# A fused decoder layer with non-local block: on VectorE the lower half of the last key unit ahead of row statistics and of the second row turn

## The chip, the cores and the metric

The kernel runs on one core of a Trainium2 chip. The metric is the device time of one execution in microseconds (us). The kernel before was timed three times: 2006.98, 2008.20 and 2008.48 us, median 2008.2 us.

## The reference

Sixteen sequences of 256 tokens with 512 features go through one decoder layer (masked self-attention, cross-attention over a second input of 256 tokens, a perceptron with 2048 hidden units), 16 heads of 32 each, and then through a non-local block. All arrays are float32.

```python
def layernorm(x, scale, bias):
    m = jnp.mean(x, axis=-1, keepdims=True)
    v = jnp.mean(jnp.square(x - m), axis=-1, keepdims=True)
    return (x - m) * jax.lax.rsqrt(v + EPS) * scale + bias
def attention(q, k, v, mask):
    scores = jnp.einsum('bhqd,bhkd->bhqk', q, k) / jnp.sqrt(jnp.float32(HD))
    scores = scores * mask - 10000.0 * (1.0 - mask)
    probs = jax.nn.softmax(scores, axis=-1)
    return jnp.einsum('bhqk,bhkd->bhqd', probs, v)
ln_out = layernorm(hidden_states, ln1_s, ln1_b)
q, k, v = jnp.split(ln_out @ w_qkv + b_qkv, 3, axis=-1)
ctx = merge_heads(attention(split_heads(q), split_heads(k), split_heads(v), ltor_mask))
x = hidden_states + ctx @ w_ao + b_ao
ln_out = layernorm(x, ln2_s, ln2_b)
q = ln_out @ w_q + b_q
k, v = jnp.split(encoder_states @ w_kv + b_kv, 2, axis=-1)
ctx = merge_heads(attention(split_heads(q), split_heads(k), split_heads(v), cross_mask))
x = x + ctx @ w_co + b_co
ln_out = layernorm(x, ln3_s, ln3_b)
x = x + gelu(ln_out @ w1 + b1) @ w2 + b2
# then, over each of the 16 sequences, a non-local block (1x1 convolutions
# theta, phi, g and w, a batch normalisation and the residual):
W = jnp.einsum('bnc,bcm->bnm', theta_x, phi_x) / phi_x.shape[-1]
y = jnp.einsum('bnm,bmc->bnc', W, g_x).transpose(0, 2, 1)
```

## The kernel before

Every float32 product is made of three: an operand is split into an upper half (names ending in `_h`, rounded by ScalarE) and a lower half (`_l`, what is left, by VectorE or GpSimd), and `product` (L66 to L68) runs high by high, high by low and low by high on TensorE.

**Bodies.** After a first stage (the folded matrices of the non-local block, up to about 80 us) the attention runs in 17 bodies, `body(r, k)` with k = 0 to 16, up to about 1265 us; then comes the perceptron, which the change does not touch. A body works on two sequences (512 tokens): bodies 0 to 7 are the self-attention of the eight pairs, 8 to 15 the cross-attention, and body 16 drains. A body has 8 slots, h = 0 to 7. Each slot carries one group of four heads through each stage of a software pipeline: the scores of one group, masking and maxima of the next older one, exponentials of the one before that, the turn of its probabilities on TensorE, their product with the values, and the division by the row sums.

**Units.** In each slot TensorE also makes two units of projection (`units_at`): in slots 0 to 3 a query unit (`q`, n = h) and a key unit (`k`, n = h), in slots 4 and 6 two value units, in slots 5 and 7 two output units of the body before. Units and weighed values take turns in two PSUM banks (`banks`). The key unit of slot h is the last unit of its slot, and its bank is the one that the first unit of slot h + 1 writes: `occupy` lets TensorE wait for `k_lo`, which VectorE counts up when it has made the lower half `k_l` (L1639), before that first product.

**Order.** Each engine runs its instructions in the order written by its own `slot` function, with semaphores between engines. In one slot (0 to 3):

- TensorE: eight transposes of probabilities (L1071, two heads), three quarters of the query unit, the turn of another head, the rest of the query unit, the key unit, scores (L1055, 24 matmuls), weighed values (L1089).
- VectorE: mask, first half (L1656, waits for the first transposes of the slot); inverse row sums, their turn, division of the weighed values (`scaled`, L1694, which writes `cx` and needs the broadcast inverses `rt` from a DMA); exponentials turned in blocks (L1686); four maxima (L1666, each with its accumulator read); mask, second half; `q_l` (L1639); four more maxima; then the tail of the slot, which the change edits: row statistics, `k_l`, row transposes.
- ScalarE: two exponentials, copies of turned probabilities, then `weighed` (L1375, waits for `scaled`), another exponential, `q_h`, five exponentials, and last `k_h` (L1299), for which `k_l` waits.
- GpSimd waits for the slot's last maximum, then makes the lower half of `cx` and, in some slots, row normalisation (L774), biases and splits.
- SyncE issues most DMAs, among them the way of the inverse row sums to DRAM and back to `rt`; ScalarE's queue carries rows, context and masks.

The row statistics of the next body (`row_statistics`, L1604, two tiles each in slots 0 and 1) are gathered by `aggregate` at the head of slot 2; GpSimd then normalises the rows in slots 2 and 3. The normalised rows of bodies 1 to 14 (`by_blocks`) are transposed in 32 x 32 blocks by VectorE (`dve.transpose` of `x[:, t, :]`, L1814), tiles 0 and 1 in slot 3 and 2 and 3 in slot 4, and written to DRAM from ScalarE's queue in slots 4 and 5 (`write_block`).

```python
    if in_bank[bank] is not None:
        sem_, per_, more_ = in_bank[bank]
        wait(pe, sem_, r * per_ + more_)
```

Of the kernel before, what the change touches and what calls it, by code (L numbers as in the profile page):

```python
# [18 lines left out]
TT = TOK // P  # L19
# [27 lines left out]
def f32(ap):  # L47

    return ap.bitcast(F32)
# [88 lines left out]
def whole_network(nc, ctx, nl, m1t_dram, inv_dram, p_dram, xt_dram, rows, x1, x2, ctx_t, s_mask, x_mask, s_weights, x_weights, fold_wt, columns,  # L138
# [12 lines left out]
    NU = 2 * NB  # L151
# [9 lines left out]
    with ExitStack() as stack:  # L161
# [27 lines left out]
        x = room.sb("x", [P, TT, H])  # L189
# [144 lines left out]
        ln_st, ln_mv, ln_ve, ln_rs, ln_x = (room.sem(n) for n in ("ln_st", "ln_mv", "ln_ve", "ln_rs", "ln_x"))  # L334
# [16 lines left out]
        a_blk, st_a, ld_a = room.sem("a_blk"), room.sems("st_a", 2), room.sems("ld_a", 2)  # L351
# [25 lines left out]
        def exists(k, h, d):  # L377
            return 0 <= NG * k + h - LAG + d < GROUPS
# [27 lines left out]
        def turns_at(k, h):  # L406

            return {6: (0, 1), 7: (2, 3)}.get(h, (None, None)) if k == 0 else (None, None)

        def by_blocks(k):  # L410

            return 0 < k < NU - 1
# [20 lines left out]
        def late(k, h):  # L433

            return (k, h) in ((0, 6), (0, 7))
# [1128 lines left out]
        def _(dve):  # L1564
            def split_raw(c, some):
                part = slice(c * H, (c + 1) * H)
                for t in some:
                    dve.wait_ge(w_hi, c * KT + t + 1)
                    hi, lo = f32(w_h[:, t, part]), w_l[:, t, part]
                    if c < 3:  # L1570
                        factor = lns_q[:, 0, t:t + 1] if c == 0 else vec(0)[:, t:t + 1]
                        dve.scalar_tensor_tensor(lo, raws[c][:, t, :], factor, hi, ALU.mult, ALU.subtract).then_inc(w_lo, 1)
                    else:
                        dve.tensor_tensor(lo, raws[c][:, t, :], hi, ALU.subtract).then_inc(w_lo, 1)
# [17 lines left out]
            def biases_of(c):  # L1592
                dve.wait_ge(folded, (c + 1) * KT)
                second, part = (1, 0) if c == 3 else (0, c)
                dve.tensor_tensor(bias_sum[:, second, part, :], shifted[:, c, :], vec(4 + c), ALU.add)\
                    .then_inc(bias_ok, 1)
                if part == 0:
                    dve.wait_ge(bias_ok, c + 1)
                    dve.tensor_scalar(bias_q[:, second, :], bias_sum[:, second, 0, :], scale, None, ALU.mult)\
                        .then_inc(bias_q_ok, 1)  # L1600

            def row_statistics(r, t):
                dve.wait_ge(ld_x[t], (r + 1) * DMA)
                last = dve.bn_stats(stats[:, t, :], x[:, t, :])  # L1604
                if t == TT - 1:
                    last.then_inc(ln_st, 1)
# [134 lines left out]
            def step(n):  # L1741
# [29 lines left out]
                if n in (7, 11, 15):  # L1771
                    biases_of((n - 7) // 4)

            def slot(r, k, h, a_, b_, own, pv):
                even, odd = turns_at(k, h)
                coming, leaves = exists(k, h, 1), exists(k, h, -2)
                if k == 0 and h == 0:
                    split_raw(2, range(KT))
                if coming:
                    mask_scores(r, k, h, 0)  # L1780
                if own:
                    inverses(r, h)
                if 0 < k < NU and h == 2:
                    aggregate(r + 1)
                bare = k == NU and h < 2
                if bare:
                    mask_scores(r, k, h, 1)
                if leaves and not late(k, h):
                    scaled(r, h, pv)
                if exists(k, h, 0) and moved(group(r, h, 0)[0]):  # L1790
                    exponentials_in_blocks(r, h)
                if coming:
                    maxima(r, k, h, 0)
                if leaves and k == NU:
                    weighed(r, k, h)
                if coming and not bare:
                    mask_scores(r, k, h, 1)
                if leaves and late(k, h):
                    scaled(r, h, pv)
                if not (k == NU and h == EARLY - 1):  # L1800
                    unit_out(a_, r, k)
                if coming:
                    maxima(r, k, h, 1)
                if even is not None:
                    rows_turned(r + (k < NU), even, tp[:, 0, :])
                    rows_turned(r + (k < NU), odd, tp[:, 1, :])
                if halves_at(k, h) is not None:
                    lower_pair(k, r, halves_at(k, h))
                if k == NU and h in (0, 2):
                    lower_pair(k - 1, r - 1, h // 2)  # L1810
                if by_blocks(k) and h in (3, 4) or k == NU - 1 and 3 <= h < 3 + TT:
                    for t in (2 * h - 6, 2 * h - 5) if by_blocks(k) else (h - 3,):
                        dve.wait_ge(ln_x, (r + 1) * TT + (t + 1))
                        dve.transpose(x[:, t, :], x[:, t, :]).then_inc(a_blk, 1)  # L1814
                if k < NU and h in ((0, 1) if k else (1, 2)):
                    row_statistics(r + 1, 0 if h == (0 if k else 1) else 2)
                    row_statistics(r + 1, 1 if h == (0 if k else 1) else 3)
                if k == 0 and h == 2:
                    aggregate(r + 1)
                if k in (2, 3) and h in (2, 4):  # L1820
                    shift_through(3 * KT + 2 * k - 4 + h // 4)
                if k == 3 and h == 5:
                    biases_of(3)
                if not (k == NU and h == EARLY):
                    for n in m_chunk_at.get((k, h), ()):
                        split_m_chunk(n)
                if k == NU and h == EARLY - 1:
                    activated(0, 0, True)
                    activated(0, 1, True)
                    unit_out(a_, r, k)  # L1830
                unit_out(b_, r, k)
                if k == 1 and h in O_SPLITS:
                    split_raw(3, O_SPLITS[h])
                for n in chunk_at.get((k, h), ()):
                    split_chunk(n)
                if k == NU and h == EARLY:
                    early_chunks = m_chunk_at[(k, h)]
                    for f in range(2, EARLY):
                        if f >= 4:
                            split_m_chunk(early_chunks[f - 4])  # L1840
                        activated(0, f, True)
                    for n in early_chunks[2:]:
                        split_m_chunk(n)
                    dve.wait_ge(m1_hi, 1)
                    dve.tensor_tensor(thw_l[:, :], m1[:, :], f32(thw_h[:, :]), ALU.subtract).then_inc(m1_lo, 1)
# [160 lines left out]
```

## Time and profile before

| | |
|---|---|
| median of three runs | 2008.2 us |
| profiled execution | 2011.13 us, of which the span 2009.3 us |
| TensorE busy | 1976.2 us (98% of the span) |
| VectorE busy | 1470.8 us (73%) |
| ScalarE busy | 1162.6 us (58%) |
| GpSimd busy | 550.2 us (27%) |
| granted TensorE clock | 0.999 over the span |

The profiled execution stands 2.9 us over the median of the runs, 1.8 us of it outside the span. The busy shares of VectorE and ScalarE are averages over two stages: in the page's 40 slices VectorE stands at 9 tenths or 8 from the third to the twenty-fifth slice (the attention) and at 3 to 6 tenths behind them. An operation's "took" overlaps the next one's start by some tens of ns, so distances are read from start to start.

### The profile page before, as it was taken

What the parts mean: (1) busy time and instruction counts of PE and PEld (TensorE: products, weight loads), DVE (VectorE), ACT (ScalarE), POOL (GpSimd) and SP (SyncE); (2) the same over time, 40 slices, a digit from 0 to 9 for tenths busy, and PEclk for the clock granted to TensorE, in tenths of its full rate; (3) what the DMA queues carried; (4) which work ended last, traced back from release to release, by engine and by line L of the source; (5) the groups of instructions that cost most, each with busy time, mean ns of one, the idle gap of its engine ahead of it and who ended that gap; (6) DMA issues with size and microseconds to landing.
All of it is one profiled execution on the core that took longest, in us unless ns stands there. A gap on an engine that the chain in (4) does not pass through costs nothing. (4 is left out here: it accounts for less than half of the span.)

```text
span 2009.3 us, 41550 instructions
## 1 busy us (share of the span) xinstructions
PE 1976.2 (98%) x13632; PEld 1570.0 (78%) x13632; DVE 1470.8 (73%) x3868; ACT 1162.6 (58%) x3251; POOL 550.2 (27%) x556
## 2 busy tenths in 40 slices
PE   9999999999999999999999998999999999999998
PEld 8877777777776777777777776888888888888887
DVE  7799999999999999899899888564444343435333
ACT  4388878888888888888888788421111121212111
POOL 1012222222224344323423432053132131313000
PEclk9999999999999999999999999999999999999999
DMA  8546667567668867767767734531212212121201
GB/s 279 168 94 139 146 165 155 128 168 161 135 173 193 195 172 173 168 162 180 176 152 183 170 90 116 171 107 35 79 42 68 68 47 78 47 63 52 61 24 48
DMA packets 681720, 252.67 MB, mean 126 GB/s; under 512 B 533312, under 2 KB 626112, under 8 KB 681536
## 3 DMA queue, kind: packets, MB, share of 16 engines
q1 hardware_dynamic: 535616, 195.84, 38.5%
q10 hardware_dynamic: 145920, 54.55, 11.2%
q8 instruction: 95, 1.56, 0.3%
q14 instruction: 89, 0.73, 0.1%
HBM read 167.41 MB, written 82.84 MB: 125 GB/s over the span
## 5 line engine op out<-in xcount | busy, mean ns | idle before, releaser
L1309 ACT ACTIVATE A_p<-A_p,A_nmax 128x256 f32<-128x256 f32 x1024 | 507.1, 500 | 5.4 <-DVE A_res L1634 1.7
L1666 DVE CUSTOM_DVE_ANT_0 A_p<-A_p,A_ma 128x256 f32<-128x256 f32 x1024 | 376.6, 423 | 4.6
L1656 DVE TENSOR_TENSOR A_p<-A_sc,A_mk 128x1024 f32<-128x1024 f32 x256 | 312.3, 1220 | 48.0 <-PE A_tp L1071 47.4
L820 POOL TENSOR_TENSOR A_ct_l<-A_cx,A_ct_h 128x256 fp32r<-128x256 f32 x122 | 114.3, 937 | 652.3 <-DVE A_nmax L1666 639.1
L1368 ACT ACTIVATE A_pt<-A_tp 128x512 f32<-128x512 f32 x396 | 218.5, 588 | 47.2 <-PE A_tp L1071 45.9
L1071 PEld LDWEIGHTS A_tp<-A_ident,A_p 128*128 128x128 f32 x1584 | 178.8, 141 | 71.2 <-ACT A_p L1309 33.0
L1071 PE MATMUL A_tp<-A_ident,A_p 128*128 128x128 f32 x1584 | 222.5, 277 | 1.5 <-DVE A_xt_l L1617 0.7
L1505 ACT ACTIVATE A_mk<-A_tp,A_cols 128x512 f32<-128x512 f32 x62 | 42.8, 690 | 269.1 <-PE A_tp L68 269.0
L1309 ACT ACTIVATION_READ_ACCUMULATOR A_p<-A_p,A_nmax 128x1 f32 x1024 | 197.2, 193 | 0.0
L1505 ACT ACTIVATE A_ma<-A_tp,A_cols 128x512 f32<-128x512 f32 x62 | 42.8, 690 | 242.5 <-PE A_tp L68 242.5
L66 PE MATMUL A_banks<-A_xt_h,A_w_h 128*128 128x512 f32 x384 | 162.2, 422 | 3.4 <-DVE A_res L1634 2.1
L929 POOL TENSOR_TENSOR A_v<-A_v,A_b_row 128x512 f32<-128x512 f32 x32 | 52.7, 1664 | 362.3 <-DMA A_v<-x 362.3
L68 PE MATMUL A_banks<-A_xt_h,A_w_l 128*128 128x512 f32 x384 | 151.1, 394 | 0.0
L67 PE MATMUL A_banks<-A_xt_l,A_w_h 128*128 128x512 f32 x384 | 150.1, 391 | 0.0
L1857 DVE CAST A_h_h<-A_ma 128x512 fp32r<-128x512 f32 x64 | 30.5, 476 | 160.4 <-ACT A_ma L1505 156.7
L1375 ACT ACTIVATE A_cx<-A_cx,A_bias_sum 128x256 f32<-128x256 f32 x128 | 65.2, 510 | 139.8 <-DVE A_cx L1694 139.7
L66 PE MATMUL A_tp<-A_xt_h,A_w_h 128*128 128x512 f32 x368 | 143.4, 390 | 0.2 <-DVE A_xt_l L1871 0.2
L67 PE MATMUL A_tp<-A_xt_l,A_w_h 128*128 128x512 f32 x368 | 143.2, 389 | 0.0
L68 PE MATMUL A_tp<-A_xt_h,A_w_l 128*128 128x512 f32 x368 | 143.2, 389 | 0.0
L1089 PE MATMUL A_banks<-A_pt,A_v 128*32 128x256 f32 x2048 | 137.9, 387 | 4.8 <-DMA A_pt<-exponentials 2.1
L1857 DVE CAST A_h_h<-A_mk 128x512 fp32r<-128x512 f32 x64 | 29.1, 454 | 143.6 <-ACT A_mk L1505 141.5
L66 PE MATMUL A_banks<-A_w_h,A_ct_h 128*128 128x512 f32 x256 | 105.7, 413 | 1.6 <-issue 1.1
(248 smaller groups left out, 5001.7 us busy)
## 6 DMA issues: line engine op xcount, KB each, us to landing
exponentials<-A_ln_shift SPq DMA_DIRECT2D x464, 64.0 KB, 2.7
A_pt<-exponentials SPq DMA_DIRECT2D x116, 256.0 KB, 3.1
A_rt<-inverses SPq DMA_DIRECT2D x512, 32.0 KB, 2.4
x<-A_res SPq DMA_DIRECT2D x64, 256.0 KB, 3.6
A_res<-x ACTq DMA_DIRECT2D x58, 256.0 KB, 4.1
turned<-A_x ACTq DMA_DIRECT2D x224, 64.0 KB, 2.8
A_x<-x SPq DMA_DIRECT2D x54, 256.0 KB, 3.7
A_x<-x ACTq DMA_DIRECT2D x42, 256.0 KB, 3.1
```

What stands on the lines that cost most here:

```text
L66: pe.matmul(out, sh, mh, start=first, stop=False)
L67: pe.matmul(out, sh, ml, start=False, stop=False)
L68: return pe.matmul(out, sl, mh, start=False, stop=last)
L820: pool.tensor_tensor(ct_l[:, f, part], cx[:, :], f32(ct_h[:, f, part]), ALU.subtract).then_inc(c_lo, 1)
L1071: last = pe.transpose(tp[:, n % 2, c * S + t * P:c * S + (t + 1) * P], p[:, g % 2, j, t, c * P:(c + 1) * P], ident[:, :])
L1089: last = pe.matmul(banks[rr, bank, 0:S], v[:, b * TPB + c, f * P + j * HD:f * P + (j + 1) * HD], turned_keys(grp, j, c), start=(c == 0), s ...
L1309: act.activation(p[:, g % 2, j, t, :], p[:, g % 2, j, t, :], ACT.Exp, scale=-1.0, bias=nmax[:, g % 2, j, t:t + 1], accum_out=rsum[:, g % 2 ...
L1368: act.activation(pt[:, moved(grp) + i, :, :], tp[:, n % 2, :].rearrange("p (c s) -> p c s", c=TPB), ACT.Copy)\
L1375: act.activation(cx[:, :], cx[:, :], ACT.Identity, bias=bias_sum[:, layer(k, h, -2), 2, f:f + 1]).then_inc(c_sum, 1)
L1505: act.activation(hf[f % 4], hidden_bank(blk, f), ACT.Gelu_apprx_tanh, bias=b1_col[:, f:f + 1])\
L1656: dve.tensor_tensor(p[:, g % 2, heads, :, :].rearrange("p j t s -> p j (t s)"), sc[:, heads, :], m, ALU.mult)\
L1666: dve.tensor_tensor_reduce(out=a_, in0=a_, in1=ma[:, b, t, :], scale=-1.0, scalar=BIG, op0=ALU.add, op1=ALU.min, accum_out=nmax[:, g % 2, ...
```

## The change

Only VectorE's order changes. In bodies 1 to 15 the two row statistics of slots 0 and 1 stand behind `k_l` instead of ahead of it. In slot 3 of bodies 1 to 14 the transpose of row tile 0 stays ahead of `k_l`, that of tile 1 goes behind it. In slot 4 the transposes of tiles 2 and 3 go behind the slot's second unit, which is a value unit and has no work on VectorE; only in body 1 do they pass something, the splits of the output weights (`split_raw`, L1574). Body 0 and body 15's row transposes are as before. No instruction is added or removed, and the four other engines keep their order.

```diff
--- before.py
+++ after.py
@@ -1771,6 +1771,11 @@
                 if n in (7, 11, 15):
                     biases_of((n - 7) // 4)
 
+            def row_blocks(r, t):
+
+                dve.wait_ge(ln_x, (r + 1) * TT + (t + 1))
+                dve.transpose(x[:, t, :], x[:, t, :]).then_inc(a_blk, 1)
+
             def slot(r, k, h, a_, b_, own, pv):
                 even, odd = turns_at(k, h)
                 coming, leaves = exists(k, h, 1), exists(k, h, -2)
@@ -1808,13 +1813,11 @@
                     lower_pair(k, r, halves_at(k, h))
                 if k == NU and h in (0, 2):
                     lower_pair(k - 1, r - 1, h // 2)
-                if by_blocks(k) and h in (3, 4) or k == NU - 1 and 3 <= h < 3 + TT:
-                    for t in (2 * h - 6, 2 * h - 5) if by_blocks(k) else (h - 3,):
-                        dve.wait_ge(ln_x, (r + 1) * TT + (t + 1))
-                        dve.transpose(x[:, t, :], x[:, t, :]).then_inc(a_blk, 1)
-                if k < NU and h in ((0, 1) if k else (1, 2)):
-                    row_statistics(r + 1, 0 if h == (0 if k else 1) else 2)
-                    row_statistics(r + 1, 1 if h == (0 if k else 1) else 3)
+                if by_blocks(k) and h == 3 or k == NU - 1 and 3 <= h < 3 + TT:
+                    row_blocks(r, h - 3)
+                if k == 0 and h in (1, 2):
+                    row_statistics(r + 1, 2 * h - 2)
+                    row_statistics(r + 1, 2 * h - 1)
                 if k == 0 and h == 2:
                     aggregate(r + 1)
                 if k in (2, 3) and h in (2, 4):
@@ -1831,6 +1834,12 @@
                 unit_out(b_, r, k)
                 if k == 1 and h in O_SPLITS:
                     split_raw(3, O_SPLITS[h])
+                if 0 < k < NU and h in (0, 1):
+                    row_statistics(r + 1, 2 * h)
+                    row_statistics(r + 1, 2 * h + 1)
+                if by_blocks(k) and h in (3, 4):
+                    for t in (1,) if h == 3 else (2, 3):
+                        row_blocks(r, t)
                 for n in chunk_at.get((k, h), ()):
                     split_chunk(n)
                 if k == NU and h == EARLY:
```

VectorE in slot 0 of body 7, from the last maxima to the next slot's `scaled`, before (`A_stats` row statistics, `A_k_l` the key unit's lower half, `A_p<-A_sc,A_mk` the next slot's mask):

```order
L1666 ISA A_p,A_nmax<-A_p,A_ma 128x256
L1666 ISA A_nmax 128x1
L1604 BN_STATS A_stats<-A_x 128x6 x2
L1639 SCALAR_TENSOR_TENSOR A_k_l<-A_banks,A_bias_sum,A_k_h 128x512
L1656 TENSOR_TENSOR A_p<-A_sc,A_mk 128x1024
L1673 RECIPROCAL A_rinv<-A_rsum 128x8
L1676 STREAM_TRANSPOSE A_turned_inv<-A_rinv 128x32
L1694 TENSOR_TENSOR A_cx<-A_banks,A_rt 128x256
```

The same place of the changed kernel:

```order
L1666 ISA A_p,A_nmax<-A_p,A_ma 128x256
L1666 ISA A_nmax 128x1
L1639 SCALAR_TENSOR_TENSOR A_k_l<-A_banks,A_bias_sum,A_k_h 128x512
L1604 BN_STATS A_stats<-A_x 128x6 x2
L1656 TENSOR_TENSOR A_p<-A_sc,A_mk 128x1024
L1673 RECIPROCAL A_rinv<-A_rsum 128x8
L1676 STREAM_TRANSPOSE A_turned_inv<-A_rinv 128x32
L1694 TENSOR_TENSOR A_cx<-A_banks,A_rt 128x256
```

The two statistics have changed places with `k_l`; the mask of the next slot still follows both.

VectorE in slot 3 of body 7, before (`A_x<-A_x` the row transposes):

```order
L1666 ISA A_p,A_nmax<-A_p,A_ma 128x256
L1666 ISA A_nmax 128x1
L1814 STREAM_TRANSPOSE A_x<-A_x 128x512 x2
L1639 SCALAR_TENSOR_TENSOR A_k_l<-A_banks,A_bias_sum,A_k_h 128x512
L1656 TENSOR_TENSOR A_p<-A_sc,A_mk 128x1024
L1673 RECIPROCAL A_rinv<-A_rsum 128x8
```

and after the change:

```order
L1666 ISA A_p,A_nmax<-A_p,A_ma 128x256
L1666 ISA A_nmax 128x1
L1777 STREAM_TRANSPOSE A_x<-A_x 128x512
L1639 SCALAR_TENSOR_TENSOR A_k_l<-A_banks,A_bias_sum,A_k_h 128x512
L1777 STREAM_TRANSPOSE A_x<-A_x 128x512
L1656 TENSOR_TENSOR A_p<-A_sc,A_mk 128x1024
L1673 RECIPROCAL A_rinv<-A_rsum 128x8
```

One transpose has gone behind `k_l`, one stays ahead of it.

## Rows read from the trace of the kernel before

**Rows 1.** Waits of the whole program: engine, line <- releaser: us, times, longest.

```profile
PEld A_banks L66 <- DVE A_k_l L1639: 10.1, 16, 1.0
...
DVE A_k_l L1639 <- ACT A_k_h L1299: 8.9, 16, 1.8
```

**Rows 2.** Timeline of VectorE, body 7, slots 0 to 3: start, took, operation, [idle].

```profile
574.18 1.28 DVE L1604 BATCH_NORM_STATS2 A_stats<-A_x 128x6 f32<-128x512 f32 x2
575.38 0.74 DVE L1639 SCALAR_TENSOR_TENSOR A_k_l<-A_banks,A_bias_sum,A_k_h 128x512 fp32r<-128x512 f32 x1
576.03 1.23 DVE L1656 TENSOR_TENSOR A_p<-A_sc,A_mk 128x1024 f32<-128x1024 f32 x1
...
585.02 1.23 DVE L1656 TENSOR_TENSOR A_p<-A_sc,A_mk 128x1024 f32<-128x1024 f32 x1
...
592.89 0.75 DVE L1639 SCALAR_TENSOR_TENSOR A_k_l<-A_banks,A_bias_sum,A_k_h 128x512 fp32r<-128x512 f32 x1 [0.47 <-ACT A_k_h L1299]
593.92 1.23 DVE L1656 TENSOR_TENSOR A_p<-A_sc,A_mk 128x1024 f32<-128x1024 f32 x1 [0.29 <-PE A_tp L1071]
...
601.44 1.30 DVE L1814 STREAM_TRANSPOSE A_x<-A_x 128x512 f32<-128x512 f32 x2
602.66 0.70 DVE L1639 SCALAR_TENSOR_TENSOR A_k_l<-A_banks,A_bias_sum,A_k_h 128x512 fp32r<-128x512 f32 x1
603.29 1.21 DVE L1656 TENSOR_TENSOR A_p<-A_sc,A_mk 128x1024 f32<-128x1024 f32 x1
```

**Rows 3.** Timeline of ScalarE, body 7, slots 0 to 2.

```profile
574.02 0.68 ACT L1299 ACTIVATE A_k_h<-A_banks,A_bias_sum 128x512 fp32r<-128x512 f32 x1
...
578.05 0.51 ACT L1375 ACTIVATE A_cx<-A_cx,A_bias_sum 128x256 f32<-128x256 f32 x1 [1.03 <-DVE A_cx L1694]
...
587.31 0.51 ACT L1375 ACTIVATE A_cx<-A_cx,A_bias_sum 128x256 f32<-128x256 f32 x1 [1.30 <-DVE A_cx L1694]
```

**Rows 4.** Timeline of TensorE, body 7: turns, and the first product after them.

```profile
575.24 1.09 PE L1071 MATMUL A_tp<-A_ident,A_p 128*128 128x128 f32 x8
576.17 0.50 PE L66 MATMUL A_banks<-A_xt_h,A_w_h 128*128 128x512 f32 x1
...
593.13 1.09 PE L1071 MATMUL A_tp<-A_ident,A_p 128*128 128x128 f32 x8
593.98 0.48 PE L66 MATMUL A_banks<-A_xt_h,A_w_h 128*128 128x512 f32 x1
...
602.03 1.09 PE L1071 MATMUL A_tp<-A_ident,A_p 128*128 128x128 f32 x8
603.42 0.50 PE L66 MATMUL A_banks<-A_w_h,A_xt_h 128*128 128x512 f32 x1 [0.30 <-DVE A_k_l L1639]
```

**Rows 5.** Timeline of TensorE, body 14, start of slot 4.

```profile
1114.46 1.09 PE L1071 MATMUL A_tp<-A_ident,A_p 128*128 128x128 f32 x8
1116.35 0.50 PE L66 MATMUL A_banks<-A_w_h,A_et_h 128*128 128x512 f32 x1 [0.79 <-DVE A_k_l L1639]
```

**Rows 6.** Timeline of VectorE, body 14, slot 3.

```profile
1108.87 0.42 DVE L1694 TENSOR_TENSOR A_cx<-A_banks,A_rt 128x256 f32<-128x256 f32 x1 [0.91 <-DMA A_rt<-inverses]
```

**Rows 7.** Timeline of TensorE: body 1, slot 5, then body 7, slot 5.

```profile
179.16 0.47 PE L66 MATMUL A_banks<-A_w_h,A_ct_h 128*128 128x512 f32 x1 [1.08 <-issue]
...
620.07 0.39 PE L1055 MATMUL A_sc<-A_k_h,A_q_h 32*128 32x256 f32 x4 [0.73 <-DVE A_p L1656]
```

**Rows 8.** Timeline of VectorE, body 15, slot 2.

```profile
1180.04 0.75 DVE L1639 SCALAR_TENSOR_TENSOR A_k_l<-A_banks,A_bias_sum,A_k_h 128x512 fp32r<-128x512 f32 x1 [0.90 <-ACT A_k_h L1299]
```

**Rows 9.** Timeline of GpSimd, body 7, slots 3 and 5.

```profile
595.22 1.53 POOL L774 TENSOR_SCALAR A_x<-A_x,A_nmean,A_rstd 128x512 f32<-128x512 f32 x2
...
616.16 1.30 POOL L831 TENSOR_TENSOR A_w_l<-A_wst,A_w_h 128x512 fp32r<-128x512 f32 x1
```

**Rows 10.** Timeline of VectorE, body 7, slot 5.

```profile
616.80 0.94 DVE L1666 CUSTOM_DVE_ANT_0 A_p<-A_p,A_ma 128x256 f32<-128x256 f32 x1
```

## The prediction

> **What bounds the kernel now.** I read the page first: TensorE is busy 98% of the span, so a change on VectorE can only act through the few us in which TensorE waits, or by making more of them. The second view is the list of waits: the weight loads of the first product of a slot waited 10.1 us in 16 places for `k_l`, the longest 1.0 us [rows 1]. That is what the moved order could win. The same list says that `k_l` itself already waits for ScalarE's `k_h` in 16 places, 8.9 us [rows 1], which is what moving it forward runs into. So the third view is the timelines of three engines side by side in one regular body (7), to see who paces whom.
>
> TensorE's first product of a slot starts 0.85 us after the slot's first turns where nothing holds it (593.13 to 593.98). By that measure it is late by 0.08 us at the start of slot 1 (575.24 to 576.17) and by 0.54 us at the start of slot 4 (602.03 to 603.42) [rows 4]. So the place where statistics are moved costs TensorE almost nothing now, and the place where a transpose is moved costs half a us.
>
> ScalarE waits 1.03 us and 1.30 us for VectorE's `scaled` in slots 1 and 2 [rows 3], and from there runs without a gap to `k_h`: from 587.31 on ScalarE to 592.89, where `k_l` starts after 0.47 us of idle time put down to `k_h`, is 5.58 us [rows 2, 3]. In slot 0 `k_h` runs from 574.02 for 0.68 us, to 574.70 [rows 3]; the maxima are over when the statistics start, at 574.18 [rows 2]. The statistics thus fill a hole of some 0.5 us that `k_l` would have to wait through anyway.
>
> **Statistics behind `k_l`, slots 0 to 2.** The pair of statistics costs 1.20 us (574.18 to 575.38), `k_l` to the next mask 0.65 us (575.38 to 576.03) [rows 2], and the mask to ScalarE's wait for `scaled` 2.02 us in slot 1 (576.03 to 578.05) and 2.29 us in slot 2 with the aggregation (585.02 to 587.31) [rows 2, 3].
> - Before, statistics and the wait for `k_h` lay beside each other. After, they stand in one line, and a loop closes between the two engines: `scaled`, 5.58 us of ScalarE, `k_l` 0.65, statistics 1.20, mask to `scaled` 2.02, in sum 9.45 us, against a slot of TensorE of 8.90 to 9.00 us (from 576.03 to 585.02 the masks are 8.99 apart [rows 2]).
> - Slot 0: `k_l` starts at 574.73 instead of 575.38, the next mask at 576.58 instead of 576.03 (+0.55).
> - Slot 1: the loop adds as much again. ScalarE gets `scaled` at 578.60, `k_l` starts at 584.18, the mask of slot 2 at 586.03 instead of 585.02 (+1.01). TensorE wins its 0.08 us at each of two slots and is otherwise untouched, since `k_l` still ends before it is asked for.
> - Slot 2 has no statistics, but everything in it is late by 1.01: `k_l` starts at 593.90 instead of 592.89 and ends at 594.65. TensorE, ready at 593.90, starts its first product of slot 3 at 594.70 instead of 593.98. **TensorE loses 0.72 us here, once per body**, where it lost nothing.
>
> **One transpose behind `k_l`, slot 3.** The two transposes cost 1.22 us (601.44 to 602.66) [rows 2], so 0.61 us goes from ahead of `k_l` to behind it. VectorE starts slot 3 at 594.55 instead of 593.92 (+0.63); `k_l` therefore starts at 602.68 against 602.66: nothing won. If slot 3's `scaled` waits for the broadcast inverses, whose DMAs are triggered in slot 2 and so come a full 1.01 late, `k_l` is late by 1.01 - 0.61 = 0.40. That wait exists: 0.91 us in body 14 [rows 6]. TensorE's own time is +0.72 less what it waits now: in body 7 0.72 - 0.54 = +0.18 us; the later of the two decides. The wait that it has now at the start of slot 4, read as in body 7, is 0.67, 0.64, 0.08, 0.21, 0.45, 0.44, 0.54, 0.83, 0.38, 1.03, 1.04, 0.56, 0.71 and 1.04 us in bodies 1 to 14 (body 14 is 1114.46 to 1116.35 less 0.85 [rows 5]); their sum of 8.6 us is most of the 10.1 of the list [rows 1].
> - Bodies 3 to 14, no late inverses: 0.72 less that wait, never under 0: 0.64 + 0.51 + 0.27 + 0.28 + 0.18 + 0.34 + 0.16 + 0.01 = +2.4 us.
> - With late inverses, never under 0.40: 0.64 + 0.51 + ten times 0.40 = +5.2 us. I take 4.7, nearer to this end, because the wait of [rows 6] is the nearest row and it grows with its trigger.
> - Body 2 I count as 0: its slot 2 carries other work of VectorE ahead of `k_l`.
>
> **What is queued behind.** VectorE starts slot 4 late by 0.65 to 1.0 (the second transpose now comes between `k_l` and the mask). ScalarE, the inverses' DMAs and GpSimd follow it. In most bodies slots 4 to 6 hide that: scores and the first product there wait for VectorE with some spare time, and I cost it at nothing; without the cover it would be up to 0.65 a body. Two bodies have no cover:
> - Body 7, slot 5: the scores already wait 0.73 us for the mask [rows 7], so VectorE's whole lateness of 0.64 to 1.04 arrives, +0.5 to +0.65 over the share counted above; I take 0.5.
> - Body 1: the first product of slot 5 already waits for the split output weights (1.08 us idle [rows 7]), made by ScalarE and then VectorE. The split now stands ahead of two transposes, which would free it 1.2 us earlier, but its upper half comes from ScalarE, which is itself 1.0 late. 0 to +1.1; I take 0.8.
>
> Body 15 keeps its transposes and gets the statistics move: in slot 2 its `k_l` already waits 0.90 us for ScalarE [rows 8], so lateness goes through. +0.7, with 0 as the other end.
>
> GpSimd's normalisation in slot 3 of body 7 ends at 596.75 [rows 9], just ahead of VectorE's maxima. Where the two meet a maximum stretches: 0.94 us at 616.80 beside a GpSimd operation that runs from 616.16 to 617.46, instead of some 0.4 [rows 9, 10]. GpSimd is late by 1.01, VectorE by 0.63 to 1.0, so at most 0.3 us of meeting, which the 0.40 above covers. The Trainium skill, "SBUF — State Buffer", in its section "SBUF: two separate sides", has an exclusive lock for this: a VectorE operation with two SBUF inputs and a GpSimd operation that reads SBUF exclude each other for the whole instruction. By that rule bodies without late inverses would lose up to 0.3 instead of 0; by a mere shared bandwidth nothing to speak of. The stretched maximum agrees with the lock.
>
> **The sum.** 4.7 + 0 + 0.5 + 0.8 + 0.7 = +6.7 us; I take +6.5. Lower bound 2.4 + 0 + 0.5 + 0 + 0 = 2.9, upper 5.2 + 0.65 + 1.1 + 0.7 = 7.7. The profiled execution would go from 2011.1 to 2017.6; it stands 2.9 us over the median of the runs, so the forecast for the median is 2008.2 + 6.5 = **2014.7 us**.
>
> **Rivals.**
> - *The wait for `k_l` simply shrinks (faster).* Were `k_h` ready when the maxima end, the wait at slot 4 would lose up to 0.61 in each of 14 bodies: with the waits above 6.9 us, plus about 0.1 a body at slots 1 and 2 and 1.0 once, 9 us in all: 1999 us. It decides as soon as ScalarE's `k_h` ends before VectorE's last maximum. For it: the list of waits names `k_l` as TensorE's largest. Against it: the 574.70 against 574.18 above, the same in slots 0 and 1 of the bodies I looked at. The Trainium skill, "Perfetto Trace Analysis", section on optimization strategy, would have one find what the gaps of the limiting engine wait for and make it start sooner. By that rule the change is right; the trace says that the thing to start sooner is `k_h`.
> - *It is hidden (no change).* The loop of 9.45 us runs for only two slots; if slot 2 had 1 us to give, TensorE would lose nothing there and slot 4's wait would shrink a little: between 2005 and 2011, say 2008. Slot 2 has 0.34 us only (592.89 + 0.75 against 593.98 [rows 2, 4]), so it needs ScalarE to catch up, which its gapless 5.58 us speak against.
> - *The lateness runs on through slots 4 to 7 (much slower).* With late masks there each body loses up to another 0.65: +10 on top, 2024 us. Against it are the waits that VectorE has there.
>
> **Chances.** Forecast 0.68, faster rival 0.08, hidden 0.17, running on 0.07. Range 2009 to 2019: the bounds 2.9 and 7.7 put the forecast's own at 2011.1 to 2015.9, and I widen it towards the hidden and the running-on case. A measurement of this kernel tells about 0.2% (4 us) from no change. Slower by more: most of the forecast's mass and the running-on case, 0.71; within it 0.21, faster 0.08.
>
> **What the changed profile would show.** Right: `k_l` in slots 0 and 1 waits about 0.5 us for `k_h`, in some 45 places instead of 16; masks of slots 1 and 2 late by 0.55 and 1.0 against TensorE's turns; a new wait of TensorE of about 0.8 us at the start of slot 3; the wait at the start of slot 4 about as late as before. Wrong: no idle time ahead of `k_l` in slot 0 (the hole was not there), or TensorE starting slot 3 0.85 us after its turns (the loop did not add up), or the wait at slot 4 gone without one at slot 3.

## The result and the profile after

The changed kernel takes 2017.4 us (median of six runs, 2015.8 to 2018.4) against 2008.1 us for the kernel before (six runs, 2007.0 to 2011.5). The ratio is 1.0038, with a 95% interval of 1.0028 to 1.0048: slower by about 7.6 us (5.6 to 9.6). The profiled execution took 2018.4 us, of which the span is 2016.6 us. TensorE's busy time went from 1976.2 to 1978.8 us, so of the 7.3 us by which the span grew 4.7 are waiting. One execution of the changed kernel with the earlier `k_h` (4534 us) and one of the kernel before beside it (2438 us) were far longer than their neighbours; they stand in no ratio below.

The list of waits of the changed kernel (engine, line <- releaser: us, times, longest):

```profile
ACT A_cx L1375 <- DVE A_cx L1694: 153.8, 123, 3.9
...
DVE A_k_l L1639 <- ACT A_k_h L1299: 23.7, 46, 1.8
...
DVE A_cx L1694 <- DMA A_rt<-inverses: 15.4, 25, 1.9
...
PEld A_banks L66 <- DVE A_k_l L1639: 10.0, 26, 0.9
...
PE A_sc L1055 <- DVE A_p L1656: 8.3, 20, 1.6
```

`k_l` waits for ScalarE's `k_h` in 46 places instead of 16 [rows 1]. TensorE's weight loads wait for `k_l` just as long in sum as before (10.0 against 10.1 us), but in 26 places instead of 16: the sum of the row did not move, its places did. Only the timelines show that. VectorE in body 7, slots 0 to 3 and the start of slot 4 (start, took, operation, [idle]); it answers to [rows 2]:

```profile
579.77 0.75 DVE L1639 SCALAR_TENSOR_TENSOR A_k_l<-A_banks,A_bias_sum,A_k_h 128x512 fp32r<-128x512 f32 x1 [0.46 <-ACT A_k_h L1299]
580.43 1.28 DVE L1604 BATCH_NORM_STATS2 A_stats<-A_x 128x6 f32<-128x512 f32 x2
581.63 1.21 DVE L1656 TENSOR_TENSOR A_p<-A_sc,A_mk 128x1024 f32<-128x1024 f32 x1
...
589.21 0.75 DVE L1639 SCALAR_TENSOR_TENSOR A_k_l<-A_banks,A_bias_sum,A_k_h 128x512 fp32r<-128x512 f32 x1 [0.47 <-ACT A_k_h L1299]
...
591.07 1.21 DVE L1656 TENSOR_TENSOR A_p<-A_sc,A_mk 128x1024 f32<-128x1024 f32 x1
...
598.90 0.75 DVE L1639 SCALAR_TENSOR_TENSOR A_k_l<-A_banks,A_bias_sum,A_k_h 128x512 fp32r<-128x512 f32 x1 [0.47 <-ACT A_k_h L1299]
...
608.13 0.71 DVE L1639 SCALAR_TENSOR_TENSOR A_k_l<-A_banks,A_bias_sum,A_k_h 128x512 fp32r<-128x512 f32 x1
608.76 0.70 DVE L1777 STREAM_TRANSPOSE A_x<-A_x 128x512 f32<-128x512 f32 x1
609.38 1.18 DVE L1656 TENSOR_TENSOR A_p<-A_sc,A_mk 128x1024 f32<-128x1024 f32 x1
```

ScalarE in the same stretch, which answers to [rows 3]:

```profile
583.63 0.51 ACT L1375 ACTIVATE A_cx<-A_cx,A_bias_sum 128x256 f32<-128x256 f32 x1 [1.45 <-DVE A_cx L1694]
...
588.50 0.67 ACT L1299 ACTIVATE A_k_h<-A_banks,A_bias_sum 128x512 fp32r<-128x512 f32 x1
...
593.33 0.51 ACT L1375 ACTIVATE A_cx<-A_cx,A_bias_sum 128x256 f32<-128x256 f32 x1 [2.21 <-DVE A_cx L1694]
```

Read together they give the loop. From the mask of slot 1 (581.63) to ScalarE's `weighed` (583.63) is 2.00 us, from there to `k_l` (589.21) 5.58, and from `k_l` to the next mask (591.07) 1.86: 9.44 us, and the mask of slot 1 to that of slot 2 is 9.44 us as well. Before it was 8.99 [rows 2]. ScalarE now waits 1.45 and 2.21 us for `scaled` instead of 1.03 and 1.30 [rows 3].

TensorE in body 7, from the turns of slot 2 to the first product of slot 4; it answers to [rows 4]:

```profile
589.29 1.09 PE L1071 MATMUL A_tp<-A_ident,A_p 128*128 128x128 f32 x8
590.14 0.48 PE L66 MATMUL A_banks<-A_xt_h,A_w_h 128*128 128x512 f32 x1
...
596.55 0.39 PE L1055 MATMUL A_sc<-A_k_h,A_q_h 32*128 32x256 f32 x4 [0.19 <-DVE A_p L1656]
...
598.46 1.09 PE L1071 MATMUL A_tp<-A_ident,A_p 128*128 128x128 f32 x8
599.71 0.50 PE L66 MATMUL A_banks<-A_xt_h,A_w_h 128*128 128x512 f32 x1 [0.15 <-DVE A_k_l L1639]
...
607.78 1.09 PE L1071 MATMUL A_tp<-A_ident,A_p 128*128 128x128 f32 x8
608.89 0.50 PE L66 MATMUL A_banks<-A_w_h,A_xt_h 128*128 128x512 f32 x1
```

Slot 2 is now 9.17 us long (589.29 to 598.46) instead of 8.90, because its scores wait for the late second mask, and the first product of slot 3 comes 1.25 us after the turns instead of 0.85. That is 0.27 + 0.40 = 0.67 us at the start of slot 3. At the start of slot 4 the distance is 1.11 us instead of 1.39 [rows 4]: 0.28 us came back. This repeats: in bodies 3 to 14 the distance at slot 3 is 1.24 to 1.30 us everywhere (0.85 before), and the excess over 0.85 at slot 4 sums to 2.7 us against 7.3 before.

From TensorE's turns, body by body, this is how much later the changed kernel is at the start of a body, in the one profiled execution of each: body 1 set to 0, body 2 +2.3, body 3 +0.9, body 7 +2.3, body 11 +4.8, body 15 +5.2, body 16 +5.4. Another 2.5 us lie ahead of body 1, where the two kernels have the same instructions, and behind the start of body 16 the changed kernel is 0.6 us shorter: 7.3 us of span in all. At the start of body 1 the ten further profiled executions stand from 0.2 us earlier to 2.9 us later than the first one of the kernel before, the unchanged kernel at +0.05, so I take the 2.5 us for chance of the execution. The unchanged kernel profiled again also had bodies 1 to 15 in 1092.7 us instead of 1095.1: against that trace the changed kernel's 1100.5 us are 7.7 us more, not 5.4. A body's term under some 0.5 us is not settled by one pair of traces unless it comes back in other bodies or kernels.

### The profile page after: what moved, and what is told of

It is laid out like the page before. It is cut to its first block and busy times, and to the rows that moved or that the text cites. A ratio compares the mean times of both kernels' runs of the same rounds, so it can differ in the third digit from the quotient of the medians.

```text
span 2016.6 us, 41550 instructions
## 1 busy us (share of the span) xinstructions
PE 1978.8 (98%) x13632; PEld 1568.8 (78%) x13632; DVE 1467.4 (73%) x3868; ACT 1160.3 (58%) x3251; POOL 549.9 (27%) x556
```

## The experiments

Ten kernels ran. The kernel before was timed beside them: median 2009.9, 2009.7 and 2009.1 us, which is what the ratios stand on; differences in us are these ratios times the 2008 us of before. The unchanged kernel run as an experiment of its own is the measure of the noise.

> The kernel before, unchanged, for the spread of its stages. In the two traces at hand the stage ahead of body 1, which has the same instructions in the same order in both, is 2.5 us longer in the changed kernel. If that is chance of an execution, it will differ by 1 to 3 us here too while the time is that of before; if it belongs to the changed kernel, this trace's body 1 starts at 131.7 us within 0.3.

Measured: 2010.0 us, ratio 0.9998 [0.9988, 1.0007]. Its body 1 starts at 131.79 us, within the 0.3 us of 131.7 that I had named as the sign against chance. By my own test the 2.5 us would belong to the changed kernel. One more execution was too small a test: over all twelve profiled executions body 1 starts between 131.5 and 134.7 us, and one of the later kernels (134.67) starts it later than the changed kernel (134.27).

### The statistics alone

```diff
-                if k < NU and h in ((0, 1) if k else (1, 2)):
-                    row_statistics(r + 1, 0 if h == (0 if k else 1) else 2)
-                    row_statistics(r + 1, 1 if h == (0 if k else 1) else 3)
+                if k == 0 and h in (1, 2):
+                    row_statistics(r + 1, 2 * h - 2)
+                    row_statistics(r + 1, 2 * h - 1)
...
+                if 0 < k < NU and h in (0, 1):
+                    row_statistics(r + 1, 2 * h)
+                    row_statistics(r + 1, 2 * h + 1)
```

> The kernel before with only the statistics of slots 0 and 1 moved behind k_l; all row transposes stay as before. My theory (a loop of 9.45 us: scaled, ScalarE to k_h, k_l, statistics, mask; VectorE late by 1.0 us in slot 2): TensorE waits about 0.8 us more for slot 3's first product, and since both transposes still stand ahead of k_l in slot 3, slot 4's first product is late by the whole lateness, 0.6 to 1.0 us in each of 14 bodies: 2008 + 9 to 14 us, about 2019 us, slower than the full change. The rival that statistics behind k_l cost nothing and the loss lies in the transposes: 2006 to 2009 us. k_l waits for k_h about 0.47 us in slots 0, 1 and 2 of nearly every body.

Measured: 2021.9 us, ratio 1.0059 [1.0046, 1.0072], +11.9 us. The waits of this kernel, and TensorE at the start of slot 4 in body 7:

```profile
DVE A_k_l L1639 <- ACT A_k_h L1299: 23.9, 46, 2.1
...
PEld A_banks L66 <- DVE A_k_l L1639: 18.5, 31, 1.0
```

```profile
609.23 1.09 PE L1071 MATMUL A_tp<-A_ident,A_p 128*128 128x128 f32 x8
611.12 0.50 PE L66 MATMUL A_banks<-A_w_h,A_xt_h 128*128 128x512 f32 x1 [0.79 <-DVE A_k_l L1639]
```

The same 46 waits for `k_h` as in the changed kernel, and the new wait at slot 3 (0.39 to 0.46 us at the first product in each of bodies 1 to 14), but nothing comes back at slot 4: here 1.89 us from the turns, and over bodies 1 to 14 the excess over 0.85 there sums to 11.5 us against 8.6 in the kernel before. The statistics are the loss.

### The transposes alone

The changed kernel with the statistics of bodies 1 to 15 back ahead of `k_l`; the transposes stay where the change put them.

```diff
-                if 0 < k < NU and h in (0, 1):
-                    row_statistics(r + 1, 2 * h)
-                    row_statistics(r + 1, 2 * h + 1)
```

> The changed kernel with the statistics put back ahead of k_l: only the second row transpose of slot 3 (and those of slot 4) is moved. My theory: k_l starts 0.5 to 0.6 us earlier in slot 3, where k_h is ready (slot 3's two transposes outlast it); TensorE's wait at the start of slot 4 shrinks by up to 0.61 us in 14 bodies, 6.9 us in all, some of it given back by the later splits: about 2002 us. The rival that the transpose behind k_l only moves the lateness into the next slot: 2006 to 2009 us.

Measured: 2003.9 us, ratio 0.9967 [0.9954, 0.9980], -6.6 us. Its list of waits has

```profile
DVE A_k_l L1639 <- ACT A_k_h L1299: 8.6, 16, 1.6
...
PEld A_banks L66 <- DVE A_k_l L1639: 2.0, 5, 1.0
```

So with the statistics in place one transpose behind `k_l` removes nearly the whole wait of slot 4: 2.0 us in 5 places instead of 10.1 in 16 [rows 1]. The two halves add to +5.3 us, against +7.6 (5.6 to 9.6) for both together, so within the noise nothing is left over.

### Is it the wait for `k_h`?

If the hole ahead of `k_l` is the cause, an earlier `k_h` must cure the changed kernel without touching VectorE. ScalarE's `k_h` goes ahead of the slot's last exponential in bodies 1 to 15:

```diff
+                ahead = b_ is not None and b_[0][0] == "k" and 0 < k < NU
                 if now:
-                    for n in (5, 6, 7):
+                    for n in (5, 6):
                         exponential(r, k, h, n)
+                    if ahead:
+                        unit_out(b_, k)
+                    exponential(r, k, h, 7)
...
-                unit_out(b_, k)
+                if not ahead:
+                    unit_out(b_, k)
```

> The changed kernel, with ScalarE making k_h ahead of its last exponential of the slot instead of behind it (bodies 1 to 15, slots 0 to 3). My theory: k_h is ready 0.49 us sooner, the loop takes 8.96 us instead of 9.45 and fits TensorE's slot; k_l's waits in slots 0 and 1 fall to about 0, TensorE's new wait at slot 3 goes, and the transposes' gain stays: 2001 to 2004 us. If the loss had another cause than the wait for k_h (statistics in the way of the next mask as such), the time stays near 2016.

Measured: 2004.9 us, ratio 0.9973 [0.9964, 0.9982], -5.4 us against before where the changed kernel has +7.6. VectorE of this kernel in body 7 (`k_l` is L1644 here, the mask L1661), behind the waits:

```profile
DVE A_k_l L1644 <- ACT A_k_h L1299: 3.5, 5, 2.0
```

```profile
571.63 0.75 DVE L1644 SCALAR_TENSOR_TENSOR A_k_l<-A_banks,A_bias_sum,A_k_h 128x512 fp32r<-128x512 f32 x1
...
573.49 1.21 DVE L1661 TENSOR_TENSOR A_p<-A_sc,A_mk 128x1024 f32<-128x1024 f32 x1
...
582.43 1.21 DVE L1661 TENSOR_TENSOR A_p<-A_sc,A_mk 128x1024 f32<-128x1024 f32 x1
```

No idle time ahead of `k_l`, and the masks are 8.94 us apart instead of 9.44: the loop is open, with the statistics still behind `k_l`. The median is 0.9 us over the 2001 to 2004 expected; the kernel before beside it was itself at 2009.9, and the ratio puts it at 2002.8 on the 2008.2 us of before. The same edit on the kernel before is the control:

> The kernel before with ScalarE's k_h ahead of its last exponential, and nothing else. My theory: in slots 0, 1 and 3 k_l stands behind statistics or transposes that outlast k_h, so nothing moves there; slot 2's wait of 0.47 us goes, where TensorE was not waiting: 2007 to 2010 us, no change against before. The rival that k_h is late everywhere and its earlier copy is a gain by itself: 2002 to 2004 us, as in the changed kernel with it.

Measured: 2008.6 us, ratio 0.9998 [0.9989, 1.0006]. There the statistics filled the hole already, so the earlier `k_h` is worth nothing; its place is worth 13.0 us in one order of VectorE and 0.4, which is nothing that can be told, in the other.

### How much filler is enough

The changed kernel with one statistic ahead of `k_l` and one behind it in slots 0 and 1:

```diff
+                if 0 < k < NU and h in (0, 1):
+                    row_statistics(r + 1, 2 * h)
...
                 if 0 < k < NU and h in (0, 1):
-                    row_statistics(r + 1, 2 * h)
                     row_statistics(r + 1, 2 * h + 1)
```

> The changed kernel with one statistic of slots 0 and 1 put back ahead of k_l and the other left behind it. My theory: the one ahead (0.6 us) fills the wait for k_h (0.47 us), the loop takes 9.45 - 0.60 = 8.85 us and fits TensorE's slot of 8.90; k_l waits for k_h hardly at all in slots 0 and 1, masks are not late, and TensorE also wins the 0.08 us at slots 1 and 2: like the turn-only kernel or 1 to 2 us less, 2001 to 2004 us. If each statistic behind k_l cost in proportion (half of the 12 us of the statistics-only kernel): about 2008 to 2010 us.

Measured: 2003.5 us, ratio 0.9970 [0.9958, 0.9982]. VectorE in body 7:

```profile
572.92 0.69 DVE L1604 BATCH_NORM_STATS2 A_stats<-A_x 128x6 f32<-128x512 f32 x1
573.53 0.73 DVE L1639 SCALAR_TENSOR_TENSOR A_k_l<-A_banks,A_bias_sum,A_k_h 128x512 fp32r<-128x512 f32 x1
574.18 0.68 DVE L1604 BATCH_NORM_STATS2 A_stats<-A_x 128x6 f32<-128x512 f32 x1
574.78 1.22 DVE L1656 TENSOR_TENSOR A_p<-A_sc,A_mk 128x1024 f32<-128x1024 f32 x1
```

One statistic (0.61 us from start to start) covers the hole of 0.47 us, and the rest of the slot is on time. Together with the earlier `k_h` nothing more is won:

> The kernel of one statistic on each side, with ScalarE's k_h ahead of its last exponential as well. My theory: the loop is already short enough, so the earlier k_h buys nothing more: within 1.5 us of that kernel, 2000 to 2004 us. If k_h still set the pace anywhere, 2 to 4 us less.

Measured: 2003.3 us, ratio 0.9969 [0.9957, 0.9981].

### One slot instead of two: a miss

The changed kernel with slot 1's statistics back ahead of `k_l`, slot 0's behind it.

```diff
+                if 0 < k < NU and h == 1:
+                    row_statistics(r + 1, 2)
+                    row_statistics(r + 1, 3)
...
-                if 0 < k < NU and h in (0, 1):
+                if 0 < k < NU and h == 0:
```

> The changed kernel with slot 1's two statistics put back ahead of k_l; slot 0's stay behind. My theory (lateness adds up once per slot with statistics behind k_l): VectorE is late by 0.55 instead of 1.01 us in slot 2, TensorE's wait at slot 3 is about 0.3 instead of 0.8 us, and the transpose moved in slot 3 outweighs it in most bodies: 2004 to 2008 us, far below the middle between the changed kernel (2017) and the turn-only kernel (2004). If the cost were simply per moved statistic, that middle: 2010 to 2011 us.

Measured: 2010.6 us, ratio 1.0003 [0.9994, 1.0012]. I expected 2004 to 2008 (the ratio makes it 2008.8 on the 2008.2 us of before); the number of the rival, 2010 to 2011, came out. VectorE was late by 0.42 us in slot 2 of body 7 where I expected 0.55, and slot 3's wait of about 0.3 us did not come: the first product there stands 0.85 us behind the turns in 13 of 14 bodies. The loss is in slot 2, where I had not looked. VectorE and then TensorE of this kernel in body 7, slots 1 and 2:

```profile
578.83 1.21 DVE L1656 TENSOR_TENSOR A_p<-A_sc,A_mk 128x1024 f32<-128x1024 f32 x1
...
587.06 0.73 DVE L1639 SCALAR_TENSOR_TENSOR A_k_l<-A_banks,A_bias_sum,A_k_h 128x512 fp32r<-128x512 f32 x1
```

```profile
586.50 1.09 PE L1071 MATMUL A_tp<-A_ident,A_p 128*128 128x128 f32 x8
587.85 0.49 PE L66 MATMUL A_banks<-A_xt_h,A_w_h 128*128 128x512 f32 x1 [0.26 <-DVE A_k_l L1639]
```

Slot 0 makes VectorE late by 0.45 us. In slot 1 `k_l` stands behind its statistics again and has no spare time (it held TensorE up by 0.08 us already in the kernel before, [rows 4]), so the first product of slot 2 comes 1.35 us after the turns: 0.5 us. It is 0.49 to 0.62 us in bodies 1 to 14 (1.03 in body 8), 7.9 us in all, and that is about the whole distance in the traces to the kernel with the transposes alone (bodies 1 to 15 in 1094.9 against 1087.0 us). A cost per moved statistic does not explain it: the kernel with one statistic on each side has two of the four behind `k_l` as well and loses nothing. In these kernels lateness costs at once where the next `k_l` has filler ahead of it (0.5 us), and a slot later where it has none, as in the changed kernel (0.67 us).

### Slot 4's transposes, and the best version

In body 1 the change also puts a split of the output weights ahead of two transposes. Both kernels here put slot 4's transposes back; the first is otherwise the one with a statistic on each side, the second the changed kernel with the earlier `k_h`.

```diff
+                if by_blocks(k) and h == 4:
+                    row_blocks(r, 2)
+                    row_blocks(r, 3)
...
-                if by_blocks(k) and h in (3, 4):
-                    for t in (1,) if h == 3 else (2, 3):
-                        row_blocks(r, t)
+                if by_blocks(k) and h == 3:
+                    row_blocks(r, 1)
```

> The kernel with one statistic on each side of k_l, and slot 4's two transposes back in their old place, ahead of the second unit and of body 1's splits; slot 3's transpose stays moved. My theory of body 1: with the transposes behind the splits VectorE stands 1.2 us waiting for ScalarE's upper half and ScalarE then 1.3 us for the transposes; put back, body 1 ends 1.1 to 1.4 us sooner than in the kernel it is made from, and no other body changes: 2001.5 to 2003 us. If body 1's loss came from the statistics, nothing changes: 2003.5 us.

> The changed kernel with ScalarE's k_h ahead of its last exponential and slot 4's transposes back in their old place. The same theory: body 1 about 1.2 us shorter than in the kernel with the earlier k_h alone, 2002 to 2004 us; the two statistics behind k_l cost nothing once k_h comes earlier, so it stands within 1.5 us of the kernel with one statistic on each side.

Measured: 2003.7 us, ratio 0.9970 [0.9957, 0.9983], and 2001.8 us, ratio 0.9966 [0.9954, 0.9978]. I expected 2001.5 to 2003 and 2002 to 2004, and neither median tells slot 4's order apart from its pair (2003.5 and 2004.9 us). The traces do: body 1 takes 73.0 us instead of 74.6, and 72.6 instead of 74.2, 1.6 us less in both pairs where I expected 1.1 to 1.4. Over all twelve kernels body 1 lasts 74.0 to 75.6 us in the six kernels with the transposes behind the split, and 72.6 to 73.3 us in five of the six that have them ahead (the sixth, with the statistics alone moved, has 74.2). Body 1, slot 4 of the changed kernel, VectorE, then ScalarE:

```profile
181.10 1.29 DVE L1574 TENSOR_TENSOR A_w_l<-A_wst,A_w_h 128x512 fp32r<-128x512 f32 x2 [1.23 <-ACT A_w_h L1268]
182.31 1.30 DVE L1777 STREAM_TRANSPOSE A_x<-A_x 128x512 f32<-128x512 f32 x2
```

```profile
183.41 0.51 ACT L1309 ACTIVATE A_p<-A_p,A_nmax 128x256 f32<-128x256 f32 x1 [1.32 <-DVE A_x L1777]
```

and the kernel with one statistic on each side and slot 4 as before:

```profile
179.12 1.30 DVE L1777 STREAM_TRANSPOSE A_x<-A_x 128x512 f32<-128x512 f32 x2
180.41 1.29 DVE L1574 TENSOR_TENSOR A_w_l<-A_wst,A_w_h 128x512 fp32r<-128x512 f32 x2
```

It is the pattern of slots 0 and 1 again: the transposes filled a wait of 1.2 us for ScalarE, and moved behind it they make the writes of ScalarE's queue and its next exponential wait 1.3 us. TensorE pays in slot 6 of body 1, at the product of weighed values. In the changed kernel, and then in the one with a statistic on each side and slot 4 moved:

```profile
199.95 1.07 PE L1089 MATMUL A_banks<-A_pt,A_v 128*32 128x256 f32 x16 [1.33 <-ACT A_v L1301]
```

```profile
197.86 1.07 PE L1089 MATMUL A_banks<-A_pt,A_v 128*32 128x256 f32 x16 [1.47 <-DMA A_pt<-exponentials]
```

A wait of 0.85 to 1.47 us stands at this product in all six kernels with slot 4's transposes moved, and in none of the six with them in their old place. In four of the six its releaser is named as the DMA that brings turned exponentials back, in the other two as ScalarE's `v`. The landing of that DMA decides it: the product starts 0.24 or 0.25 us after it in all six, while in the six kernels without the wait the product starts 1.2 us before the same `v` is done, so it does not need it. The path there can be followed in the traces. VectorE, late behind the split, turns the next exponentials 5.1 us after the start of slot 5 instead of 3.9 to 4.1, and SyncE issues their stores from 5.8 us on instead of 4.6 to 4.8. It issues the load at 11.9 to 12.2 us instead of 10.7 to 11.1, and the load takes 7.0 to 7.5 us instead of 5.4 to 6.9. Why it takes longer is not shown. The next four stores, issued while it is under way, are also spread over 4.2 to 5.1 us in the six and over 2.1 to 3.0 us in the others.

The version to keep is the last one, the changed kernel with `k_h` one exponential earlier and slot 4 as it was: -6.8 us (-9.2 to -4.4) on the kernel before. It has the lowest median, but its interval overlaps those of the five other kernels that stand at -5.4 to -6.6 us.

## Why the prediction was right

- **The statistics fill a hole: right.** `k_l` waits 0.46 and 0.47 us for `k_h` in slots 0 and 1, in 46 places against some 45 forecast. The experiments show it as the cause: take away the wait (`k_h` earlier, or one statistic ahead) and 13.0 to 13.6 us of the changed kernel's time go.
- **The loop of 9.45 us: right.** It measures 9.44 us in both slots of body 7, and in those of bodies 2 to 4 too; its terms were 5.58, 0.66, 1.20 and 2.00 against 5.58, 0.65, 1.20 and 2.02.
- **TensorE loses 0.72 us at slot 3: right in size, in two parts.** I had one wait of about 0.8 us at the first product. It came as 0.27 us at slot 2's scores, which wait for the late second mask, and 0.40 at the first product; slots 2 and 3 together grew by 0.53 to 0.81 us in bodies 4 to 14 (body 8 apart, where a shift from slots 0 and 1 falls in).
- **Slot 4's wait "about as late as before": wrong, though not by the sum.** It shrank in every body, from 7.3 to 2.7 us over bodies 3 to 14. In the formula "the later of the two decides" that is the 0.72 less the wait of now, with late inverses a rest of 0.40. The rests I read are 0 to 0.44 us, in bodies 8 to 14 from 0.19 to 0.44. My 0.40 in ten bodies was near the upper edge, and so was 4.7 as the value taken. Between the two ends I had chosen the right branch: `scaled` of slot 3 waits for the inverses in 13 of the bodies 1 to 14 (0.35 to 1.26 us each) instead of in 8, so they do come late. But they do not come a full 1.01 late everywhere: in bodies 10, 11 and 14 `scaled` starts only 0.2 to 0.4 us later against the turns. Bodies 3 to 14 with body 7's slot 5 were forecast at 4.7 + 0.5 = 5.2 and came to 4.3 us.
- **Body 7, slot 5: +0.5 forecast; the size came, the path was wrong.** Slot 5 takes 11.05 us instead of 10.51. But the scores wait 0.73 us for the mask as before; what grew is the wait of the second output unit's first product for `cx`. TensorE before, then after:

```profile
616.31 0.50 PE L66 MATMUL A_banks<-A_w_h,A_ct_h 128*128 128x512 f32 x1 [0.52 <-DVE A_cx L1694]
```

```profile
622.36 0.50 PE L66 MATMUL A_banks<-A_w_h,A_ct_h 128*128 128x512 f32 x1 [0.96 <-DVE A_cx L1694]
...
626.10 0.39 PE L1055 MATMUL A_sc<-A_k_h,A_q_h 32*128 32x256 f32 x4 [0.73 <-DVE A_p L1656]
```

Nor is it the lateness that the statistics cause: the kernel with the statistics alone moved has 10.47 us in this slot, and all eight kernels with slot 3's transpose moved have 10.90 to 11.08, also those without late statistics. It goes with slot 3's transpose standing between `k_l` and the next mask; the way from there to `cx` of slot 5 is not followed here. That the number fits is luck.
- **Body 1: +0.8 forecast, +2.3 in the trace.** This term was too small. 0.5 us is the ordinary loss at slots 3 and 4, which I had not counted for this body. Most of the other 1.9 is the product of slot 6 that waits 1.33 us, by the landing times for a transfer. I had followed the split to the first product of slot 5 and bounded it by 1.1; what it did to the transfers behind it I had not looked at. My description ahead of the prediction, that slot 4's transposes pass something only in body 1, is also incomplete: in bodies 2 and 3 they pass `shift_through` (L1589) too.
- **Body 2: 0 forecast, -1.3 in the trace.** Its slot 4 lost its wait of 0.64 us, and slots 2 and 3 are 0.45 shorter. In the unchanged kernel profiled again that wait is 0.08 us, and it has none of the 0.47 at slot 3 that the first trace has. So most of the -1.3 is what one execution happens to have. That it sets off what body 1 had too much is luck.
- **Body 15: +0.7 forecast, +0.2 in the trace; the term itself is right.** Slot 3 of this body takes 10.18 us instead of 9.40, and its first product waits 0.62 us for `k_l`. The kernel with the statistics alone moved has the same 10.18, the unchanged kernel profiled again the same 9.40, and the others 9.30 to 9.57. The sum is small because slot 0 was 0.41 us shorter, and that slot varies from 9.02 to 9.79 us over the twelve traces.
- **The sum.** +6.5 us forecast; the medians say +7.6 (5.6 to 9.6), the traces +5.4 from body 1 to body 16, or +7.7 against the unchanged kernel profiled again. The forecast lies inside that interval. The loop, its cost at slot 3 and body 15's term carry it. That the whole comes so near is in part luck, since body 1 was too small by 1.5 us, bodies 3 to 14 with body 7's slot 5 were too large by 0.9, body 2 brought -1.3 that was not forecast, and two traces of one kernel differ by 2.4 us over these bodies. The miss in size that repeats from kernel to kernel is body 1's.
- **The rivals.** *The wait simply shrinks* would have been 1999 us. It holds for the transposes alone (-6.6) and is decided where I said: once `k_h` ends just before the maxima do (571.60 against 571.65 us in slot 0 of body 7), the changed kernel is at 2004.9, which is -5.4 us and not the rival's -9. *Hidden* is out by the 1.24 us at each slot 3. *Runs on* is out: from slot 4's first product on, bodies 3 to 14 gave +1.5 us in all, of which bodies 6, 7 and 14 are 1.4.
- **GpSimd meeting VectorE in slot 3: it did not happen.** I had allowed at most 0.3 us. In slots 2 and 3 of bodies 1 to 14 of the changed kernel no maximum runs beside a normalisation: in body 7 the last normalisation ends 0.2 us before the first maximum starts, and every maximum of slot 3 takes 0.38 to 0.42 us. So the term is nothing, and the quoted rule on the exclusive lock is neither confirmed nor contradicted by the change.

Where the gain went that moving `k_l` forward seems to promise: in slots 0 and 1 there was only 0.08 us to win, and behind `k_l` the statistics pushed everything else back by some 0.5 us a slot (9.44 us against 8.99 and 8.90). In slot 3, where there was half a us to win, 1.0 us of inherited lateness ate it.

## What to carry to other kernels

Before an operation is moved behind a waiting one, read whether it lies in the time that the waiting one waits: if the waiting instruction's own operand (`k_h`) ends after the filler starts, the move buys nothing and puts the filler into the line. Where engines release each other in a ring, add up one turn of the ring from start to start (9.45 us) and set it against the slot of the limiting engine (8.90 to 9.00): an excess adds up from slot to slot and is paid where the spare time ends. A change with two halves is worth taking apart, since one half was worth -6.6 us under the +11.9 of the other.

## What was not expected of the hardware

- The row statistic takes 0.61 us from start to start for a tile of 128x512, whichever side of `k_l` it stands on (572.92 to 573.53, and 574.18 to 574.78), and ring times repeat to a few hundredths of a us: in the changed kernel the mask of slot 1 starts 9.43 to 9.49 us after that of slot 0 in bodies 1 to 14 (body 8 apart, with 10.84), and the mask of slot 2 9.44 or 9.45 us after that of slot 1.
- The time before body 1 with equal instructions differs by up to 3.2 us between profiled executions (from 0.2 us earlier to 2.9 us later than the first), far more than any ring above. A term that rests on one body in one trace needs a second execution beside it.
- The releaser that the profile names varies between kernels that wait in one place: for the product of body 1, slot 6, it is four times the DMA of exponentials and twice ScalarE's `v`. The landing time of the load settles what the name does not: the product starts 0.24 or 0.25 us after it in all six. What the wait has in common (slot 4's transposes moved, a load that lands later) was seen only over twelve traces.
